# Key features from three full-height stacks a tile, and key norms given to ScalarE as a bias, in a random-feature attention block

## The chip, the cores and the metric

The kernel runs on one core of a Trainium2 chip. The metric is the time of one execution on the device in microseconds; 1303.4 us is the median of 3 runs of the kernel before (1302.08 to 1303.77). Traces are of one profiled execution.

## The reference

For each of 8 batches of 1024 tokens (512 channels, 16 heads of 32):

```python
def feature_map(x, orf):                       # orf: 128 x 32
    proj = x @ orf.T / d_k ** 0.25
    norm = jnp.sum(x * x, axis=-1, keepdims=True) / (2.0 * math.sqrt(d_k))
    return (jnp.exp(proj - norm) + EPS) / math.sqrt(m)
q = feature_map(split(x @ Wq.T + bq), orf)     # per head
k = feature_map(split(x @ Wk.T + bk), orf)
v = split(x @ Wv.T + bv)
kv, ksum = jnp.einsum('nlm,nld->nmd', k, v), jnp.sum(k, axis=1)
out = jnp.einsum('nlm,nmd->nld', q, concat(kv, ksum))
out = out[..., :-1] / out[..., -1:]
x = layernorm(x + merge(out) @ Wo.T + bo)
x = layernorm(x + x @ (ternary(weight) * scale).T)
```

The change touches only how `proj - norm` of the keys is formed.

## The kernel before

Every operand of a product is split into a rounded part (hi) and the rest (lo); a product is hi·hi + hi·lo + lo·hi, summed in PSUM.

A batch is worked off in 8 units and an output part. Unit `u` holds 4 heads (128 channels): even units are keys, odd ones queries. A key unit and the query unit behind it are called a pair below. All engines walk the same list, `SCHEDULE`, each taking the stages that concern it, in order and with semaphores between them. The stages that matter here:

- `P` (TensorE, L980): the projection of a unit two ahead, in parts of 6 products of 512 columns. A key unit has four parts: two before its middle, one behind it, one at its end.
- `S` (ScalarE, L668 and L670): writes the hi part of a projected half unit into `EH` ("unit_hi") and its squares. `L` (VectorE, L845) writes the lo part into `EL`. `Q` (VectorE, L853 and L857) turns and sums the squares; `N` (L863 to L868) makes norm rows of them.
- `LIFT` (SyncE's queue): copies the 32-row pieces of `EH` and `EL` from SBUF to SBUF into a stack, `ST`, which has one slot for keys and one for queries: 10 transfers for keys (L517, L523, L528), 12 for queries. The hi ones wait for `S` of the second half (L500) and for the last `F` of the unit before the last (L499), the lo ones for `L` (L525).
- `NL` (GpSimd's queue, L584 and L589): copies the norm rows into the same stack: 4 transfers for keys, 2 for queries.
- `F` (TensorE, called from L994 for keys with the product on L943, L999 for queries): the features of one tile. A key tile (128 tokens, 4 heads, 512 columns of one PSUM bank) is four products of 256 columns: for each pair of heads one against `MA` with 128 rows and one against `MB` with 68 rows, of which 4 carry the norms with a factor of -1. It goes round three PSUM banks, so `F` of a tile waits for the exponential of the tile three before. ScalarE (L687) takes the whole tile, 128x512, with one exponential into `FE`. `G` (TensorE, L1012) multiplies features by values, `KVT` and `GG` make use of the sums. VectorE also adds up the features (L809).
- `XT` (ScalarE, L655): splits the next batch's x, eight tiles, within unit 5. `LX` (SyncE, L439) loads those tiles; tiles 0 to 4 in unit 2, tiles 5 to 7 in unit 5. `LR` (SyncE, L461) loads rows of x.
- `ST` (ScalarE, L635 and L725): second layer norm and store of an output tile. Two of these lie in unit 0.

In a key unit other than 0 the list says, with the unit's own number `u`: `F` 0, 1; `P`; `F` 2, 3; `P`; `S` and `L` of the first half of unit `u+2`; `F` 4, 5; `Q`; `G` 0 to 3; `P`; `F` 6, 7; `S`, `L`, `Q` of its second half; `N`; `LIFT` and `NL` of unit `u+2`; `P`. In unit 2 the `LX` of five tiles stand behind that; in unit 5 those of three tiles stand behind the `LIFT` and `NL` of unit 6, which unit 4 ends with.

Of the kernel before, what the change touches and what calls it, by code (L numbers as in the profile page):

```python
# [44 lines left out]
P = 128  # L45
# [8 lines left out]
A_SQ = math.sqrt(1.0 / (2.0 * math.sqrt(DH)) / C_EXP)  # L54
QK = 3 * DH + 2
WARM = 24
KK = 2 * DH + 4
# [184 lines left out]
def attention_kernel(nc, x, xt, wq, wk, wv, wo, wff, bias, bo, orf, out):  # L242
# [5 lines left out]
    with ctx:  # L248
# [9 lines left out]
        ST = sb("stacks", [P, 2, 4 * L], F32R)  # L258
# [10 lines left out]
        MA = sb("orf_key_a", [P, 2 * M], F32R)  # L269
        MB = sb("orf_key_b", [P, 2, 2 * M], F32R)  # L270
# [4 lines left out]
        NN = sb("norm_rows", [P, 2, 2, DH], F32R)  # L275
# [48 lines left out]
        v_xlo, v_plo, v_n = Signal("x_lo_ready", 4, 4), Signal("unit_lo_ready", 2 * NU), Signal("norms_ready", 3 * NU, 2)  # L324
# [54 lines left out]
        masks = KVS[:, 0:2, :].rearrange("p a (b m) -> p (a b) m", m=M)  # L379
# [17 lines left out]
        def turned_rows(b, t):  # L397

            if b + 1 < B:
                return ST[:, 1, 2048:2560], ST[:, 1, 2560:3072]  # L400
            return last_hi[:, t, :], last_lo[:, t, :]
# [31 lines left out]
        def _(sp):  # L433
# [29 lines left out]
            for kind, b, at, _, _ in steps():  # L463
# [30 lines left out]
                elif kind == "LIFT":  # L494
                    u = at[0]
                    slot = ST[:, u % 2, :].bitcast(F32)
# [4 lines left out]
                    if u == 1:  # L501
# [10 lines left out]
                        continue  # L512
                    for h in range(HG):
                        src = hi[DH * h:DH * (h + 1), :]
                        if is_key(u):
                            r, c = 2 * DH * (h % 2), L * (h // 2)
                            sp.dma_start(slot[r:r + DH, c:c + L], src).then_inc(sig.sem, 16)  # L517
                        else:
                            sp.dma_start(slot[0:DH, L * h:L * (h + 1)], src).then_inc(sig.sem, 16)
                            sp.dma_start(slot[2 * DH:3 * DH, L * h:L * (h + 1)], src).then_inc(sig.sem, 16)  # L520
                    if is_key(u):
                        for p in range(2):
                            sp.dma_start(slot[0:2 * DH, L * (2 + p):L * (3 + p)],  # L523
                                         hi[2 * DH * p:2 * DH * (p + 1), :]).then_inc(sig.sem, 16)
                    wait(v_plo.sem, v_plo.nth(b, 2 * u + 2))  # L525
                    for h in range(HG):
                        r, c = (2 * DH * (h % 2) + DH, L * (h // 2)) if is_key(u) else (DH, L * h)
# [3 lines left out]
        def _(pool):  # L531
# [14 lines left out]
            for t in (WQS, MA, MB):  # L546
                last = nc.gpsimd.memset(t[:].bitcast(F32), 0.0)
# [567 lines left out]
```

## Time and profile before

| | us |
|---|---|
| median of 3 runs | 1303.4 |
| lowest and highest | 1302.08, 1303.77 |
| span of the profiled execution | 1300.4 |

The profiled execution's span runs from its first to its last instruction; its own time beyond it isn't recorded, and the median is 3.0 us above that span. The share of an engine's busy time says little here, since the work is a chain of stages with different limits. The profile is read in this order: the chain that ended last, for the engine that sets the end; the stretches from the start of one key unit's exponentials to the next one's; and then each engine's and each DMA queue's instructions in one such stretch in order of time.

### The profile page before, as it was taken

What the parts mean: (1) busy time and instruction counts of PE and PEld (TensorE: products, weight loads), DVE (VectorE), ACT (ScalarE), POOL (GpSimd) and SP (SyncE); (2) the same over time, 40 slices, a digit from 0 to 9 for tenths busy, and PEclk for the clock granted to TensorE, in tenths of its full rate; (3) what the DMA queues carried; (4) which work ended last, traced back from release to release, by engine and by line L of the source; (5) the groups of instructions that cost most, each with busy time, mean ns of one, the idle gap of its engine ahead of it and who ended that gap; (6) DMA issues with size and microseconds to landing.
All of it is one profiled execution on the core that took longest, in us unless ns stands there. A gap on an engine that the chain in (4) does not pass through costs nothing.

```text
span 1300.4 us, 24924 instructions
## 1 busy us (share of the span) xinstructions
PE 1280.2 (98%) x8626; PEld 965.9 (74%) x8626; DVE 942.1 (72%) x1784; ACT 702.1 (54%) x1403; POOL 384.1 (30%) x685
## 2 busy tenths in 40 slices
PE   9999999999999999999999999999999999999987
PEld 8767787777877678776787768876788767887665
DVE  7599765886668875787657786587875787657876
ACT  5557435564355743657336663367534665446534
POOL 1213432125311343214421234312352123422143
PEclk9999999999999999999999999999999999999999
DMA  7668414773146821567215762258612686026711
GB/s 242 140 136 217 95 50 111 170 190 84 57 118 160 200 68 54 133 159 189 62 57 130 182 165 69 62 130 197 162 45 71 142 209 149 30 80 147 163 51 65
DMA packets 83773, 160.56 MB, mean 123 GB/s; under 512 B 19648, under 2 KB 37184, under 8 KB 83136
## 3 DMA queue, kind: packets, MB, share of 16 engines
q1 hardware_dynamic: 67856, 139.78, 43.4%
q10 hardware_dynamic: 9648, 16.85, 3.4%
q0 software_dynamic: 6144, 2.34, 2.1%
q8 instruction: 69, 1.13, 0.4%
q14 instruction: 56, 0.46, 0.1%
HBM read 39.13 MB, written 16.78 MB: 43 GB/s over the span
## 4 chain that ended last, share of the span: by engine, by line
PE 84%; DVE 6%; ACT 6%; issue 3%; DMA 1%; POOL 0%; SPq 0%; ACTq 0%; DVEq 0%; POOLq 0%
PE ps L943 28%; PE ps L980 25%; PE ps L1044 8%; PE ps L1012 4%; PE ps L966 4%; PE ps L968 4%; PE ps L967 4%; PE ps L999 4%; ACT features L687 2%; PE ps L1070 2%; ACT x_hi L655 1%; DMA rows<-in_Wk_t 1%; DVE squares_turned L853 1%; ACT unit_hi L668 0%; DVE cols L857 0%
## 5 line engine op out<-in xcount | busy, mean ns | idle before, releaser
L687 ACT ACTIVATE features<-ps 128x512 f32<-128x512 f32 x512 | 279.0, 603 | 254.4 <-PE ps L943 196.0
L584 POOL DMA_DIRECT2D stacks<-norm_rows x128 | 86.3, 681 | 305.7 <-DVE norm_rows L868 185.8
L943 PE MATMUL ps<-Wo_hi,stacks 128*128 128x512 f32 x448 | 150.4, 402 | 0.0
L660 ACT ACTIVATE values_then_attention<-ps 128x512 f32<-128x512 f32 x64 | 38.3, 598 | 197.2 <-PE ps L968 194.1
L809 DVE TENSOR_TENSOR den<-den,features 128x512 f32<-128x512 f32 x186 | 128.0, 688 | 12.7
L562 POOL TENSOR_SCALAR stats<-stats 128x1 f32<-128x1 f32 x128 | 36.1, 282 | 323.4 <-DVE stats L796 323.2
L943 PE MATMUL ps<-orf_key_a,stacks 128*128 128x256 f32 x512 | 131.4, 288 | 0.1
L943 PE MATMUL ps<-orf_key_b,stacks 68*128 68x256 f32 x512 | 128.2, 282 | 0.0
L1044 PE MATMUL ps<-features,kv_ksum 128*32 128x512 f32 x1024 | 123.1, 598 | 3.4 <-ACT features L687 2.1
L845 DVE SCALAR_TENSOR_TENSOR unit_lo<-ps,cols,unit_hi 128x512 fp32r<-128x512 f32 x128 | 94.2, 736 | 35.0 <-ACT squares L670 34.9
L943 PEld LDWEIGHTS ps<-orf_key_a,stacks 128*128 128x128 f32 x512 | 97.1, 190 | 25.9 <-issue 22.1
L943 PE MATMUL ps<-W_ternary,stacks 128*128 128x512 f32 x448 | 110.7, 389 | 0.0
L980 PE MATMUL ps<-x_hi,Wk_hi 128*128 128x512 f32 x256 | 106.5, 416 | 1.4 <-DVE x_lo L838 1.4
L966 PE MATMUL ps<-Wv_hi,x_hi 128*128 128x512 f32 x256 | 102.6, 401 | 1.0 <-DVE unit_lo L845 0.2
L943 PEld LDWEIGHTS ps<-Wo_hi,stacks 128*128 128x128 f32 x448 | 84.1, 188 | 24.4 <-issue 7.1
L635 ACT ACTIVATE rows<-rows,stats 128x512 f32<-128x512 f32 x112 | 88.0, 813 | 26.4 <-POOL stats L566 25.6
L980 PE MATMUL ps<-x_lo,Wq_hi 128*128 128x512 f32 x256 | 101.3, 396 | 0.0
L980 PE MATMUL ps<-x_hi,Wq_hi 128*128 128x512 f32 x256 | 100.9, 394 | 0.0
L980 PE MATMUL ps<-x_hi,Wq_lo 128*128 128x512 f32 x256 | 100.7, 393 | 0.0
L980 PE MATMUL ps<-x_hi,Wk_lo 128*128 128x512 f32 x256 | 100.7, 393 | 0.0
L980 PE MATMUL ps<-x_lo,Wk_hi 128*128 128x512 f32 x256 | 100.4, 392 | 0.0
L967 PE MATMUL ps<-Wv_lo,x_hi 128*128 128x512 f32 x256 | 99.9, 390 | 0.0
(141 smaller groups left out, 2773.2 us busy)
## 6 DMA issues: line engine op xcount, KB each, us to landing
stacks<-unit_hi SPq DMA_DIRECT2D x384, 128.0 KB, 2.4
stacks<-unit_lo SPq DMA_DIRECT2D x256, 128.0 KB, 3.7
stacks<-unit_hi SPq DMA_DIRECT2D x64, 256.0 KB, 3.9
out<-rows ACTq DMA_DIRECT2D x56, 256.0 KB, 2.0
rows<-in_x_t SPq DMA_DIRECT2D x49, 256.0 KB, 4.5
rows<-in_x SPq DMA_DIRECT2D x32, 256.0 KB, 4.3
features<-in_x SPq DMA_DIRECT2D x32, 256.0 KB, 4.2
values_then_attention<-in_x_t SPq DMA_DIRECT2D x8, 256.0 KB, 7.1
```

Of the source, the lines that this page charges most:

```text
L584: pool.dma_start(slot[row:row + 2, c:c + L].rearrange("o (t c) -> o t c", c=DH), NN[2 * DH * p:2 * DH * (p + 1), u % 2, part, :].bitcast(F ...
L635: nc.scalar.activation(row, row, ACT.Identity, scale=ln(k, t, 10), bias=ln(k, t, 11))\
L687: nc.scalar.activation(FE[:, n % 8, :, 0:M], ps[:, :].rearrange("p (a m) -> p a m", a=HG), ACT.Exp, scale=C_EXP).then_inc(a_exp.sem, 1)
L809: ins = nc.vector.tensor_tensor(total, total, FE[:, r, :, 0:M], ALU.add)
L845: nc.vector.scalar_tensor_tensor(out=EL[:, u % 2, half], in0=ps[:, :], scalar=BC[:, u:u + 1], in1=EH[:, u % 2, half].bitcast(F32), op0=ALU ...
L943: last = mm(out, a, b, start=(n == 0), stop=(n == len(terms) - 1))
L966: mm(ps[:, :], XH[:, k, c], WH["v"][:, k, :], start=(k == 0), stop=False)
L967: mm(ps[:, :], XH[:, k, c], WL["v"][:, k, :], start=False, stop=False)
L968: last = mm(ps[:, :], XL[:, k, c], WH["v"][:, k, :], start=False, stop=(k == KT - 1))
L980: last = mm(ps[:, :], *terms[n], start=(n == 0), stop=(n == len(terms) - 1))
L999: last = mm(ps[:, :], WQS[0:QK, h, :], slot[0:QK, c:c + HALF], start=True, stop=True)
L1044: last = mm(bank[DH * h:DH * (h + 1), :], KVS[:, g % 2, c + DH * h:c + DH * (h + 1)], FE[:, HG * half + h, :, 0:M], start=True, stop=True, ...
```

## The change

The stack `ST` becomes two tensors, `KST` (3 x 1024 columns, keys) and `QST` (4 x 1024, queries). The twelve pieces that a key tile needs (hi, lo and hi again of four heads) are laid in three full stacks of 128 rows, and a tile takes three products of 256 columns against `MK`, whose outputs overlap by 128 columns. The norm rows of the keys leave the stack. `Q` of a key unit sums the squares with a minus sign into `KN`; `N` and GpSimd's `NL` are gone for keys. In their place SyncE's queue copies the sums by 16 transfers of 32 partitions x 8 numbers (32 bytes each) into `NB`, at the place of `NL`. ScalarE waits for these ahead of the first exponential of a key unit, and takes each tile by four exponentials of 128 columns, with a column of `NB` as bias. `A_SQ` becomes `A_KEY` for keys, since the norm is no longer scaled by `C_EXP`. Setup has fewer masks. `LIFT` of keys has 9 transfers instead of 10.

```diff
-        KEY_LIFTS, QUERY_LIFTS = 10, 12
+        KEY_LIFTS, QUERY_LIFTS = 9, 12
...
-        KEY_NORMS, QUERY_NORMS = 4, 2
+        KEY_NORMS, QUERY_NORMS = 16, 2
...
+                    if is_key(u):
+                        for n, r, h, k in ((0, 2 * DH, 0, 2), (1, DH, 1, 2), (2, 0, 2, 2), (0, 0, 0, 1), (2, 3 * DH, 3, 1)):
+                            sp.dma_start(slot[r:r + DH * k, L * n:L * (n + 1)], hi[DH * h:DH * (h + k), :]).then_inc(sig.sem, 16)
+                        wait(v_plo.sem, v_plo.nth(b, 2 * u + 2))
+                        for h, (n, r) in enumerate(((0, DH), (1, 0), (1, 3 * DH), (2, 2 * DH))):
+                            sp.dma_start(slot[r:r + DH, L * n:L * (n + 1)], lo[DH * h:DH * (h + 1), :]).then_inc(sig.sem, 16)
+                        continue
...
+                elif kind == "NL" and is_key(at[0]):
+                    u = at[0]
+                    wait(v_ns.sem, v_ns.nth(b, 2 * u + 2))
+                    if b or u:
+                        wait(a_exp.sem, a_exp.nth(b, 8 * (u - 1)))
+                    for h in range(HG):
+                        for a in range(4):
+                            sp.dma_start(NB[DH * a:DH * (a + 1), TT * h:TT * (h + 1)], KN[DH * h:DH * (h + 1), a, :]).then_inc(n_lifted[0].sem, 16)
...
-                if kind == "NL":
+                if kind == "NL" and not is_key(t):
                     lift_norms(b, t)
...
-                    nc.scalar.activation(FE[:, n % 8, :, 0:M], ps[:, :].rearrange("p (a m) -> p a m", a=HG),
-                                         ACT.Exp, scale=C_EXP).then_inc(a_exp.sem, 1)
+                    if is_key(u):
+                        if r == 0:
+                            norms_lifted(act, b, u)
+                        for h in range(HG):
+                            last = nc.scalar.activation(FE[:, n % 8, h, 0:M], ps[:, M * h:M * (h + 1)], ACT.Exp,
+                                                        bias=NB[:, TT * h + r:TT * h + r + 1], scale=C_EXP)
+                        last.then_inc(a_exp.sem, 1)
+                    else:
+                        nc.scalar.activation(FE[:, n % 8, :, 0:M], ps[:, :].rearrange("p (a m) -> p a m", a=HG),
+                                             ACT.Exp, scale=C_EXP).then_inc(a_exp.sem, 1)
...
+                    if is_key(u):
+                        if h == 0:
+                            norms_lifted(dve, b, u - 2)
+                        by_tile = KN[:, :, 4 * h:4 * (h + 1)].rearrange("p a t -> p t a")
+                        nc.vector.reduce_sum(by_tile, blocks.rearrange("p (t a) c -> p t a c", a=4),
+                                             axis=mybir.AxisListType.X, negate=True).then_inc(v_ns.sem, 1)
...
-                elif kind == "N":
+                elif kind == "N" and not is_key(u):
...
                     if is_key(u):
-                        for p in range(2):
-                            at_a, at_b = L * p + P * r, L * (2 + p) + P * r
-                            last = products(ps[:, 256 * p:256 * (p + 1)], [(slot[:, at_a:at_a + P], MA[:, :]),
-                                                                          (slot[0:KK, at_b:at_b + P], MB[0:KK, p, :])])
+                        for n in range(3):
+                            last = mm(ps[:, M * n:M * (n + 2)], KST[:, L * n + P * r:L * n + P * (r + 1)], MK[:, n, :],
+                                      start=(n == 0), stop=(n == 2), skip_group_check=True)
```

## Rows read from the trace of the kernel before

**Rows 1.** Page: busy time and share of the span; then the chain by engine
```profile
PE 1280.2 (98%) x8626; PEld 965.9 (74%) x8626; DVE 942.1 (72%) x1784; ACT 702.1 (54%) x1403; POOL 384.1 (30%) x685
...
PE 84%; DVE 6%; ACT 6%; issue 3%; DMA 1%; POOL 0%; SPq 0%; ACTq 0%; DVEq 0%; POOLq 0%
```

**Rows 2.** Stretches: A:B, length; busy PE, PEld, DVE, ACT, POOL; clock; DMA share; GB/s
```profile
524.92:547.46 22.54, 22.54 (x190) 16.00 (x189) 16.58 (x30) 15.58 (x33) 5.34 (x9) 1.00 0.63 144
547.46:571.24 23.78, 23.78 (x196) 17.05 (x195) 19.05 (x37) 14.25 (x31) 3.84 (x6) 1.00 0.71 175
571.24:596.56 25.32, 24.82 (x200) 17.71 (x199) 21.61 (x41) 18.45 (x40) 7.54 (x9) 1.00 0.75 183
596.56:620.39 23.83, 23.78 (x192) 16.80 (x190) 19.66 (x40) 15.89 (x35) 7.85 (x10) 1.00 0.59 146
...
1205.93:1229.43 23.50, 22.61 (x190) 16.07 (x189) 19.30 (x40) 14.27 (x32) 3.84 (x6) 1.00 0.66 142
```

**Rows 3.** Chain of waits in order, key unit 2: start us, length us, what
```profile
551.63 0.96 PE ps L943 x8
...
556.15 2.77 PE ps L980 x12
```

**Rows 4.** ScalarE in order of time, unit 2: start us, length us, instruction, idle before
```profile
547.46 1.09 ACT L687 ACTIVATE features<-ps 128x512 f32<-128x512 f32 x2 [3.96 <-PE ps L943]
...
556.68 0.69 ACT L668 ACTIVATE unit_hi<-ps,cols 128x512 fp32r<-128x512 f32 x1
557.25 0.70 ACT L670 ACTIVATE squares<-ps,cols 128x512 f32<-128x512 f32 x1
...
560.95 0.37 ACT L697 ACTIVATE kv_ksum_t<-ps,cols 128x128 f32<-128x128 f32 x1
561.22 0.19 ACT L697 ACTIVATION_READ_ACCUMULATOR kv_ksum_t<-ps,cols 128x1 f32 x1
```

**Rows 5.** SyncE's queue in order of time, units 2 to 5 (SPq: issue of transfers)
```profile
557.46 2.42 SPq L517 DMA_DIRECT2D stacks<-unit_hi  x4
...
561.26 2.87 SPq L528 DMA_DIRECT2D stacks<-unit_lo  x4
...
567.50 0.51 SPq L519 DMA_DIRECT2D stacks<-unit_hi  x1
...
585.04 2.90 SPq L528 DMA_DIRECT2D stacks<-unit_lo  x4
588.05 2.70 SPq L439 DMA_DIRECT2D rows<-in_x_t  x3
```

**Rows 6.** Page: DMA issues, KB each, median us to landing
```profile
stacks<-unit_hi SPq DMA_DIRECT2D x384, 128.0 KB, 2.4
```

**Rows 7.** VectorE, end of unit 4's squares (second half)
```profile
559.81 0.69 DVE L857 TENSOR_REDUCE cols<-squares_turned 128x16 f32<-128x512 f32 x1
```

**Rows 8.** ScalarE in order of time, unit 0 of the same batch
```profile
528.39 0.81 ACT L635 ACTIVATE rows<-rows,stats 128x512 f32<-128x512 f32 x1
...
529.77 1.09 ACT L687 ACTIVATE features<-ps 128x512 f32<-128x512 f32 x2 [0.57 <-PE ps L943]
```

**Rows 9.** ScalarE in order of time, last split of the next x, end of unit 5
```profile
596.02 0.63 ACT L655 ACTIVATE x_hi<-rows 128x512 fp32r<-128x512 f32 x1 [0.65 <-DMA rows<-in_x_t]
596.56 1.07 ACT L687 ACTIVATE features<-ps 128x512 f32<-128x512 f32 x2
```

**Rows 10.** ScalarE's own queue: issues of 32-byte rows at the start, and of a store
```profile
1.50 0.45 ACTq L621 DMA_DIRECT2D cols<-in_bias_columns  x1
1.98 0.45 ACTq L622 DMA_DIRECT2D den<-in_orf_t  x1
...
486.05 0.34 ACTq L725 DMA_DIRECT2D out<-rows  x1
```

**Rows 11.** ScalarE in order of time, the last key unit of the last batch
```profile
1229.43 3.05 ACT L687 ACTIVATE features<-ps 128x512 f32<-128x512 f32 x6 [3.12 <-PE ps L943]
```

**Rows 12.** A stretch near the end, columns as in rows 2: granted clock
```profile
1283.50:1293.00 9.50, 7.89 (x30) 6.13 (x31) 6.06 (x11) 4.51 (x7) 2.90 (x8) 0.82 0.15 55
```

More of the change, by code:

```diff
@@ L513, in _ @@
                     for h in range(HG):
                         src = hi[DH * h:DH * (h + 1), :]
[L515 to L520, printed above, removed]
@@ L578, in lift_norms @@
                     wait(t_ff.sem, t_ff.nth(b, 0))
-                wait(v_n.sem, v_n.nth(b, 3 * u + 3))
+                wait(v_n.sem, v_n.nth(b, 3 * (u // 2) + 3))
                 for part in range(2):
-                    if is_key(u):
-                        for p in range(2):
-                            row, c = 2 * DH + 2 * part, L * (2 + p)
-                            pool.dma_start(slot[row:row + 2, c:c + L].rearrange("o (t c) -> o t c", c=DH),
-                                           NN[2 * DH * p:2 * DH * (p + 1), u % 2, part, :].bitcast(F32))\
-                                .then_inc(n_lifted[0].sem, 16)
-                    else:
-                        row = 3 * DH + part
-                        pool.dma_start(slot[row:row + 1, :].rearrange("o (t c) -> o t c", c=DH),
-                                       NN[:, u % 2, part, :].bitcast(F32)).then_inc(n_lifted[1].sem, 16)
+                    row = 3 * DH + part
+                    pool.dma_start(slot[row:row + 1, :].rearrange("o (t c) -> o t c", c=DH),
+                                   NN[:, part, :].bitcast(F32)).then_inc(n_lifted[1].sem, 16)
             for kind, b, at, _, _ in steps():
                 t = at[0] if at else 0
-                if kind == "NL":
+                if kind == "NL" and not is_key(t):
                     lift_norms(b, t)
@@ L755, in constant_rows @@
                         nc.vector.tensor_copy(WQS[DH * r:DH * (r + 1), h, :], wT[DH * r:DH * (r + 1), 0:M])
-                for r in range(4):
-                    a = r // 2
-                    nc.vector.tensor_copy(MA[DH * r:DH * (r + 1), M * a:M * (a + 1)], wT[DH * r:DH * (r + 1), 0:M])
+                for n, r, a in ((0, 0, 0), (0, 1, 0), (0, 3, 1), (1, 0, 0), (1, 2, 1), (1, 3, 1), (2, 1, 1), (2, 2, 1)):
+                    nc.vector.tensor_copy(MK[DH * r:DH * (r + 1), n, M * a:M * (a + 1)], wT[DH * r:DH * (r + 1), 0:M])
                 link(nc.vector.tensor_copy(rounded, wT[:, 0:M]))
@@ L763, in constant_rows @@
                     nc.vector.tensor_tensor(WQS[r, h, :], wT[r, 0:M], rounded[r, :].bitcast(F32), ALU.subtract)
-                for p in range(2):
-                    for a in range(2):
-                        r = slice(DH * a, DH * (a + 1))
-                        nc.vector.tensor_tensor(MB[r, p, M * a:M * (a + 1)], wT[r, 0:M], rounded[r, :].bitcast(F32), ALU.subtract)
-                nc.vector.tensor_copy(WQS[3 * DH:QK, :, :], masks[3 * DH:QK])
-                last = nc.vector.tensor_copy(MB[2 * DH:KK, :, :].rearrange("p a (b m) -> p (a b) m", b=2), masks[2 * DH:KK])
-                last.then_inc(s_orf, 1)
+                for n, q, a in ((0, 2, 0), (1, 1, 0), (2, 0, 0), (2, 3, 1)):
+                    r = slice(DH * q, DH * (q + 1))
+                    nc.vector.tensor_tensor(MK[r, n, M * a:M * (a + 1)], wT[r, 0:M], rounded[r, :].bitcast(F32), ALU.subtract)
+                nc.vector.tensor_copy(WQS[3 * DH:QK, :, :], minus_one).then_inc(s_orf, 1)
             def weight_scale():
@@ L998, in _ @@
                         c = L * h + HALF * half
-                        last = mm(ps[:, :], WQS[0:QK, h, :], slot[0:QK, c:c + HALF], start=True, stop=True)
+                        last = mm(ps[:, :], WQS[0:QK, h, :], QST[0:QK, c:c + HALF], start=True, stop=True)
                     last.then_inc(t_f.sem, 1)
```

76 lines of the change are left out of this document (36 added, 40 removed).

## Prediction

> **What bounds the kernel now.** I read the chain of waits by engine first: TensorE is on it for 84% of the span and busy for 98% [rows 1], so in most stretches a product taken away moves the end. Then I read the stretches from one key unit's first exponential to the next one's: TensorE is busy for all 23.78 us of the second, ScalarE for 14.25, and only in the third does TensorE wait a little, behind the splitting of x [rows 2]. Last I followed one key unit on ScalarE and on SyncE's queue in order of time [rows 4, 5]. The reader is to see there that ScalarE has room and that SyncE's queue, which no busy column shows, issues one transfer per 0.6 us: 4 in 2.42 us [rows 5]. That queue is what the change loads.
>
> **TensorE, removed.** Two key tiles, 8 products of 256 columns, take 0.96 us on the chain [rows 3], 0.12 us a product. Three instead of four saves 0.12 us a tile, 0.96 us a key unit, and over 8 batches x 4 key units x 8 tiles 30.7 us, if TensorE still sets the pace. The overlapping outputs change no column count.
>
> **ScalarE, added.** One exponential of 128x512 is replaced by four of 128x128 with a bias column. Two whole ones take 1.09 us, so about 0.50 us a tile [rows 4]. The trace has no 128-column exponential; nearest is the 128x128 activation with a bias column, behind which the next instruction starts 0.27 us later (560.95 to 561.22) [rows 4]. The 512-column one with bias is followed after 0.57 us (556.68 to 557.25) [rows 4]; taking the share of 384 columns off it, at 0.50/512 us a column, leaves 0.20 us. I take 0.26, near the row of the same size: 1.04 us a tile, 8.3 a key unit instead of 4.0. Bounds: 0.20 and 0.30. In unit 2 ScalarE's work in a pair goes from 14.25 to about 18.6 us of 23.78 [rows 2], so it fits on average; in unit 0 two stores lie there too, each holding ScalarE from 528.39 to 529.77 [rows 8].
> The Trainium skill ("ScalarE: Activation LUTs", What ACT_TABLE_LOAD costs) gives about 280 ns + 0.833 ns a column with a pointer bias and an overlap of 93 ns, which for 128 columns is an estimate of 0.29 us apart, near my upper bound; by it the time below would be about 23 us higher.
>
> **VectorE and GpSimd, removed.** `N` of keys (three small instructions) and GpSimd's four transfers a key unit go. Neither is on the chain beyond a few per cent [rows 1], so I cost them at nothing. The sum with a minus sign has the same 512 inputs; nothing there.
>
> **SyncE's queue, added, and the new wait.** `LIFT` of keys loses one transfer (0.61 us), and 16 follow it for the norms. They stand ahead of the `LX` transfers and of the query unit's `LIFT` (12 transfers, 7.3 us), and ScalarE's exponentials of the key unit wait for the last of them; behind that wait stand all of ScalarE's work, then the three PSUM banks, then TensorE. What does one cost? The trace has no such small SBUF-to-SBUF transfer on this queue. Lifts cost 0.51 alone and 0.61 in a train (2.42 for 4, and the gap) [rows 5]; 128 rows of 32 bytes on ScalarE's queue 0.45, 0.48 apart; a store of 256 KB 0.34 [rows 10]. Size thus doesn't order these prices, kind of transfer may: I take the lifts' 0.62, with 0.36 (a store and a gap) as the low end and 0.68 as the high. Landing: 2.3 us from the issue as for a lift [rows 6].
>
> **The loop that this closes.** Set 0 at the first exponential of key unit u (2 or 4), where it had been waiting. Eight tiles, 8.3 us, and `S` of the first half, 1.14, come ahead of `S` of the second half, whose hi part ends 0.69 after its start: 10.15. In the kernel before that start lay at 9.2 (547.46 to 556.68), and the queue began 0.1 after the hi part [rows 4, 5]. `LIFT` took 6.67 us for 10 transfers (557.46 to 561.26 + 2.87) [rows 5]; 9 take 6.06, so 16.3. The sums are ready sooner: 3.8 us behind the start of `S` before (556.68 to 559.81 + 0.69) [rows 4, 7], so at 13.3. Fifteen distances of 0.62 and one landing, 9.3 + 2.3, and 0.2 for the semaphores: 28.1 us until the first exponential of unit u+2. The pair took 23.78 before, and would take 22.8 by TensorE. So the saved 0.96 us vanishes and 4.3 us are added, in an idle TensorE.
>
> **By pairs of a batch.**
> - Unit 0 to 2: two tiles, `S`, two tiles, a store, one tile bring 7.6 us; tile 7 gets its bank and is done at about 8.2, then one more tile and `S` end at 9.4. Hence 9.5 + 6.06 + 11.8 = 27.3 against 22.54 [rows 2]: +4.8.
> - Unit 2 to 4: +4.3.
> - Unit 4 to 6: 28.1 isn't the end here. The `LX` of tiles 5 to 7 come behind the norms: 10.25 + 6.06 + 9.9 + 0.2 = 26.4 after the start. Before, the exponentials of unit 6 followed their issue by 8.5 us (588.05 to 596.56, behind the last split of x) [rows 5, 9]. So 34.9 against 25.32 [rows 2]: +9.6. The five `LX` of unit 2 push unit 5's `LIFT` by 3 us, which ends inside this.
> - Unit 6 to the next batch: no key unit waits there for norms before the output part is over. TensorE's saving is eaten by the late start, the rest has cover: 0.
> That is 18.7 us a batch, for 7 batches 131. The last has no x to load: 4.8 + 4.3 + (28.1 - 23.50 = 4.6) [rows 2], and its last key unit, where six exponentials take 3.05 us in a row [rows 11], adds some 3.5 net: 17. The first batch's norms (16 behind `LIFT` 0) are done in the prologue, under the projections. The sum is 148 us: span 1300.4 + 148 = 1448.4, and with the 3.0 us by which the median lies above the span 1451 us.
>
> **The clock.** TensorE will stand for 4 to 9 us ahead of three key units a batch. Near the end of the trace, after gaps, the granted clock was 0.82 over 9.5 us, that is 1.2 GHz instead of 2.4 for 3.4 of them, a loss of 1.7 us [rows 12]. After each wait ScalarE, not TensorE, sets the pace, so I take nothing; if each of the 24 waits cost 1.7, it would be 41 us.
>
> **Rivals.**
> 1. *Small transfers are cheap to issue.* At 0.36 us apart a train is 3.9 us shorter: pairs of +0.9, +0.4, +5.5, and 6 in the last batch: 53 us, 1357. For it: the 0.34 of a store; against it: each SBUF-to-SBUF issue in the trace took over 0.5.
> 2. *The norms arrive in time,* by landing alone. Then unit 0 is held by ScalarE: with 1.04 us a tile TensorE waits for banks there some 3 us in all (a store between tiles 3 and 4), +2.0, and three pairs gain 0.96 or less: about 1303. The loop allows this if it is under 22.8, that is if a distance is under 0.27 us.
> The Trainium skill ("DMA: Bandwidth & Descriptors", Issuing engines are not separate DMA queues) calls the issue time "usually small relative to the DMA itself"; by that rule the train would cost hardly more than one landing, which is this rival. The rows stand against it: 0.6 us each, times 16, is four times a landing.
> 3. *Faster, as the removal of products promises.* Same point, 0.27 us a distance, and a short exponential at 0.20, so that unit 0 keeps up: all 30.7 us come in, 1273. Against it: no queue row is under 0.33.
> 4. *Worse than the loop:* 0.68 a distance (+0.9 a loop), 0.30 an exponential (+0.04 x 32, 1.3 a loop) and the clock's 1.7 a wait together: 1451 + 24 x 3.9 = 1545; two of the three, 1490 to 1520.
>
> **How the numbers follow.** Forecast 0.68 (1395 to 1490: distance 0.45 to 0.68, a short exponential 0.24 to 0.30), rival 1 0.14 (1345 to 1395), rival 2 0.05, rival 3 0.04, rival 4 0.09. Leaving out rivals 2 to 4 leaves out 0.18, so the range is 1345 to 1490. Differences under 0.2%, 2.6 us, can't be told from none: faster 0.06 (rival 3 and a part of 2), same 0.03, slower 0.91.
>
> **What would show it.** In the trace after: three products a key tile, 0.36 us a tile; 16 transfers a key unit on SyncE's queue, 0.6 us apart; ScalarE's idle time ahead of the first key exponential ended by DMA, 4 to 9 us; first exponentials of units 2 and 4 some 28 us apart, of 4 and 6 some 35; the output part as long as before. TensorE busy share well under 98%. It's wrong if the distances are under 0.45 us, if key exponentials are over 0.3 apart, or if ScalarE's waits end by TensorE.

## The result and the profile after

The changed kernel took 1474.9 us (median of 4 runs, 1470.3 to 1477.7), the kernel before, run beside it, 1303.6 us: a ratio of 1.1315 [1.129, 1.1339]. The forecast was 1451, with a range from 1345 to 1490.

Page of the kernel after: span, busy time, the chain by engine and by line, the costliest group, and the issues of the new transfers. To be read against [rows 1]. A line number is always that of the kernel whose profile is shown, so one and the same instruction has other numbers in other kernels.

```profile
span 1475.4 us, 25377 instructions
...
PE 1305.1 (88%) x8370; PEld 969.1 (66%) x8370; DVE 942.7 (64%) x1692; ACT 833.8 (57%) x2171; POOL 294.8 (20%) x553
...
PE 52%; SPq 24%; ACT 10%; issue 5%; DMA 4%; DVE 3%; ACTq 0%; POOL 0%; POOLq 0%; DVEq 0%
PE ps L951 16%; SPq L534 15%; PE ps L988 11%; ACT features L687 7%; SPq L515 5%; PE ps L1001 4%; PE ps L974 4%; PE ps L976 4%; PE ps L975 4%; SPq L518 4%; PE ps L1019 2%; DMA key_bias<-key_norms 2%; DMA rows<-in_x_t 2%; PE ps L1051 2%; PE ps L1077 2%
...
L687 ACT ACTIVATE features<-ps,key_bias 128x128 f32<-128x128 f32 x1024 | 277.4, 422 | 209.3 <-DMA key_bias<-key_norms 145.8
...
key_bias<-key_norms SPq DMA_DIRECT2D x512, 1.0 KB, 1.7
```

TensorE has 256 products fewer and is busy for 25 us more. Its share of the chain fell from 84% to 52%, and SyncE's queue, which was at 0%, has 24%, of which 15 are the norm transfers (L534) and 9 the key lifts (L515, L518). ScalarE stood for 145.8 us ahead of key exponentials until a norm transfer landed.

Stretches of the kernel after, the same batch as [rows 2]; the first three run from one key unit's first exponential to the next one's, the fourth is key unit 6 with half of unit 7, the fifth the output part. The last two lines lie around the wait of unit 4.

```profile
590.08:618.25 28.17, 24.79 (x192) 16.64 (x190) 19.76 (x36) 19.56 (x58) 2.92 (x6) 1.00 0.35 92
618.25:648.36 30.11, 24.56 (x186) 17.35 (x186) 19.39 (x34) 18.36 (x56) 1.70 (x4) 0.92 0.50 110
648.36:684.12 35.76, 25.54 (x186) 17.71 (x186) 21.52 (x37) 22.66 (x63) 3.77 (x3) 0.83 0.63 166
684.12:708.46 24.34, 23.11 (x178) 16.11 (x178) 17.27 (x27) 20.00 (x59) 5.28 (x5) 0.92 0.55 147
708.46:771.57 63.11, 63.00 (x294) 51.63 (x294) 37.99 (x73) 21.82 (x36) 23.52 (x51) 1.00 0.21 61
636.00:649.00 13.00, 8.00 (x54) 4.12 (x53) 8.53 (x18) 2.79 (x7) 1.07 (x2) 0.93 0.19 40
649.55:656.00 6.45, 6.45 (x50) 5.43 (x51) 3.52 (x5) 6.36 (x22) 0.00 (x0) 0.66 1.00 261
```

The three pairs take 28.2, 30.1 and 35.8 us where [rows 2] have 22.5, 23.8 and 25.3; the forecast had 27.3, 28.1 and 34.9. From the first exponential of unit 6 to that of the next batch it is 87.45 us (24.34 + 63.11), before it was 87.07 in that batch. TensorE's clock, 1.00 in all of [rows 2], is 0.92, 0.83 and 0.92 in the stretches behind a wait.

The 16 norm transfers of a key unit, which SyncE issues in a row, are called the train below. One loop in order of time, SyncE's queue between the first exponentials of units 2 and 4, to be read against [rows 5]:

```profile
629.53 3.46 SPq L515 DMA_DIRECT2D key_stack<-unit_hi  x5
633.11 2.47 SPq L518 DMA_DIRECT2D key_stack<-unit_lo  x4
635.77 10.88 SPq L534 DMA_DIRECT2D key_bias<-key_norms  x16
646.77 1.93 SPq L439 DMA_DIRECT2D rows<-in_x_t  x4
```

And ScalarE in the same loop, to be read against [rows 4] (in brackets the idle time before, and what ended it):

```profile
618.25 4.23 ACT L687 ACTIVATE features<-ps,key_bias 128x128 f32<-128x128 f32 x16 [7.56 <-DMA key_bias<-key_norms]
...
626.69 2.17 ACT L687 ACTIVATE features<-ps,key_bias 128x128 f32<-128x128 f32 x8 [0.99 <-PE ps L1001]
628.70 0.74 ACT L664 ACTIVATE unit_hi<-ps,cols 128x512 fp32r<-128x512 f32 x1
...
648.36 4.23 ACT L687 ACTIVATE features<-ps,key_bias 128x128 f32<-128x128 f32 x16 [10.21 <-DMA key_bias<-key_norms]
```

The loop closes as foretold: exponentials, the hi part at 628.70, nine lifts from 629.53, sixteen norm transfers from 635.77, landing, exponentials at 648.36. Sixteen exponentials in 4.23 us with the last 0.42 long lie (4.23 - 0.42)/15 = 0.254 us apart.

### The profile page after: what moved, and what is told of

Read it like the earlier page. It is cut to its first block, busy times and chain, and to the rows that moved or that the text cites. A ratio compares the mean times of both kernels' runs of the same rounds, so it can differ in the third digit from the quotient of the medians.

```text
span 1475.4 us, 25377 instructions
## 1 busy us (share of the span) xinstructions
PE 1305.1 (88%) x8370; PEld 969.1 (66%) x8370; DVE 942.7 (64%) x1692; ACT 833.8 (57%) x2171; POOL 294.8 (20%) x553
## 3 DMA queue, kind: packets, MB, share of 16 engines
q1 hardware_dynamic: 91920, 140.33, 37.3%
## 4 chain that ended last, share of the span: by engine, by line
PE 52%; SPq 24%; ACT 10%; issue 5%; DMA 4%; DVE 3%; ACTq 0%; POOL 0%; POOLq 0%; DVEq 0%
PE ps L951 16%; SPq L534 15%; PE ps L988 11%; ACT features L687 7%; SPq L515 5%; PE ps L1001 4%; PE ps L974 4%; PE ps L976 4%; PE ps L975 4%; SPq L518 4%; PE ps L1019 2%; DMA key_bias<-key_norms 2%; DMA rows<-in_x_t 2%; PE ps L1051 2%; PE ps L1077 2%
## 5 line engine op out<-in xcount | busy, mean ns | idle before, releaser
L687 ACT ACTIVATE features<-ps,key_bias 128x128 f32<-128x128 f32 x1024 | 277.4, 422 | 209.3 <-DMA key_bias<-key_norms 145.8
L1001 PE MATMUL ps<-orf_key,key_stack 128*128 128x256 f32 x768 | 141.1, 318 | 139.6 <-ACT features L687 139.6
L1001 PEld LDWEIGHTS ps<-orf_key,key_stack 128*128 128x128 f32 x768 | 125.1, 216 | 179.1 <-ACT features L687 146.8
L691 ACT ACTIVATE features<-ps 128x512 f32<-128x512 f32 x256 | 139.8, 618 | 21.9 <-PE ps L1006 17.8
L951 PE MATMUL ps<-Wo_hi,query_stack 128*128 128x512 f32 x448 | 150.3, 402 | 0.0
L585 POOL DMA_DIRECT2D query_stack<-norm_rows x64 | 35.3, 554 | 445.6 <-DVE norm_rows L876 389.2
L951 PE MATMUL ps<-W_ternary,query_stack 128*128 128x512 f32 x448 | 110.7, 389 | 0.0
L988 PE MATMUL ps<-x_lo,Wk_hi 128*128 128x512 f32 x256 | 110.3, 431 | 0.0
L951 PEld LDWEIGHTS ps<-Wo_hi,query_stack 128*128 128x128 f32 x448 | 84.1, 188 | 24.4 <-issue 7.1
L976 PE MATMUL ps<-Wv_hi,x_lo 128*128 128x512 f32 x256 | 99.9, 390 | 0.0
```

The lines of the kernel that those rows point to most:

```text
L687: last = nc.scalar.activation(FE[:, n % 8, h, 0:M], ps[:, M * h:M * (h + 1)], ACT.Exp, bias=NB[:, TT * h + r:TT * h + r + 1], scale=C_EXP)
L691: nc.scalar.activation(FE[:, n % 8, :, 0:M], ps[:, :].rearrange("p (a m) -> p a m", a=HG), ACT.Exp, scale=C_EXP).then_inc(a_exp.sem, 1)
L951: last = mm(out, a, b, start=(n == 0), stop=(n == len(terms) - 1))
L976: last = mm(ps[:, :], XL[:, k, c], WH["v"][:, k, :], start=False, stop=(k == KT - 1))
L988: last = mm(ps[:, :], *terms[n], start=(n == 0), stop=(n == len(terms) - 1))
L1001: last = mm(ps[:, M * n:M * (n + 2)], KST[:, L * n + P * r:L * n + P * (r + 1)], MK[:, n, :], start=(n == 0), stop=(n == 2), skip_group_ch ...
```

## The experiments

Each time is the median of 4 to 10 runs, beside runs of the kernel before, whose median there was between 1302.8 and 1303.4. "Pairs" below are the three stretches from key unit to key unit in the fourth of the 8 batches, and from unit 6 to the next batch, in this order; before they are 22.54, 23.78, 25.32 and 87.07, after 28.17, 30.11, 35.76 and 87.45. The last two are best read as a sum: in five of the first seven batches of the kernel before they are 24.6 and 87.8, with the same 112.4 together. The code cuts are against the changed kernel unless another is named, and `...` marks lines left out.

The theory is the forecast's: a place on SyncE's queue is the price, by the wait for the last norm and by what stands behind the train. Its rivals: ScalarE's short exponentials, the landing of a transfer, TensorE's clock. The first three kernels add the parts of the change one by one.

**1. Three products alone.** The norms, their transfers and the four short exponentials go.

```diff
-                    for h in range(HG):
-                        for a in range(4):
-                            sp.dma_start(NB[...], KN[...]).then_inc(n_lifted[0].sem, 16)
...
-                        for h in range(HG):
-                            last = nc.scalar.activation(FE[:, n % 8, h, 0:M], ps[:, M * h:M * (h + 1)], ACT.Exp,
-                                                        bias=NB[:, TT * h + r:TT * h + r + 1], scale=C_EXP)
+                        nc.scalar.activation(FE[:, n % 8, :, 0:M], ps[:, :].rearrange("p (a m) -> p a m", a=HG),
+                                             ACT.Exp, scale=C_EXP).then_inc(a_exp.sem, 1)
```

> The stacks and three products of the change alone: one exponential of 512 columns a key tile as before, no norm transfers, no wait. The key norms are left out of the computation. Theory A (the products are worth what TensorE's chain says, and the loss is all in what came with them): 0.96 us a key unit, 30.7 us in all, 1273 us; a little less where the splitting of the next x sets unit 5, 1273 to 1281. Rival B (the three overlapping products are themselves slower, or TensorE loses elsewhere): 1300 or more.

Measured: 1288.3 us, ratio 0.9881 [0.9865, 0.9897], 14.5 us under before and outside what was expected. Pairs 21.80, 22.80, 23.61 and 88.46. The first two give 0.7 and 1.0 us. The last two together took 112.4 us before and 112.1 here, so they give 0.3 where twice 0.96 had been reckoned. What is lost there is taken up in 5.

**2. With the four short exponentials,** bias zero, no transfers. As in 1, SyncE's branch for the key norms is gone too.

```diff
-                        if r == 0:
-                            norms_lifted(act, b, u)
```

> As the run of three products alone, but each key tile takes four exponentials of 128 columns with a bias column that is zero from the start; the key norms are left out of the computation. Nothing is transferred and nothing waits. Theory A: only unit 0, where two stores lie, is held by ScalarE (about 3 us a batch), and the last key unit: about 1303, 1295 to 1310. Rival C (the doubled work of ScalarE is a main cause of the loss): 1340 or more.

Measured: 1313.7 us, 1.008 [1.0062, 1.0097], 25.4 more than the kernel in 1 and 4 us over what was expected. Pairs 24.47, 22.80, 23.61 and 88.59: short exponentials cost nothing in pairs two and three, as the forecast had it, and 2.7 us in the first, where two output stores also lie on ScalarE (3.3 in the first batch, where ScalarE splits a weight there instead). The last key unit of all has 2.8 more (9.6 instead of 6.8 us to the query's first exponential).

**3. With the transfers, unwaited.** The kernel of 2 with all 16 transfers a key unit, into a tile that nobody reads.

```diff
+        NB2 = sb("unread_bias", [P, HG * TT])
...
-                            sp.dma_start(NB[...], KN[...]).then_inc(n_lifted[0].sem, 16)
+                            sp.dma_start(NB2[...], KN[...]).then_inc(n_lifted[0].sem, 16)
```

> As the run with short exponentials and a zero bias (key norms left out of the computation), but SyncE's queue also issues the 16 small transfers at their place, into a tile that nobody reads; ScalarE doesn't wait for them. It tells the time that they take in the queue from the wait for them. Theory A (the queue is full: what stands behind the 16, the query unit's 12 lifts and the loads of x, comes late too): pairs of units 2 and 4 together 12 us longer, about 1400, 1375 to 1425. Rival D (it is ScalarE's wait for the last small transfer alone): as without them, about 1303.

Measured: 1427.9 us, 1.0949 [1.0924, 1.0974]. So 114.2 us come from the train's place on the queue alone, with no wait for a norm, and the wait adds only the last 46 or so, to 1474.9. The shares hold in this order of adding: where the queue sets the pace, it covers what the short exponentials cost in 2. Stretches of this kernel:

```profile
572.45:596.93 24.48, 22.79 (x182) 15.03 (x181) 16.35 (x27) 19.61 (x58) 2.48 (x5) 1.00 0.40 105
596.93:623.90 26.97, 24.52 (x188) 16.92 (x187) 18.48 (x34) 18.36 (x55) 1.06 (x2) 0.94 0.52 120
623.90:658.99 35.09, 27.00 (x198) 18.61 (x196) 24.08 (x45) 22.72 (x63) 4.86 (x5) 0.90 0.65 168
```

ScalarE in order of time in pairs two and three, its waits for query features:

```profile
610.77 1.09 ACT L693 ACTIVATE features<-ps 128x512 f32<-128x512 f32 x2 [3.00 <-PE ps L1008]
...
641.10 1.09 ACT L693 ACTIVATE features<-ps 128x512 f32<-128x512 f32 x2 [6.35 <-PE ps L1008]
```

SyncE's queue in pair three:

```profile
642.28 10.45 SPq L535 DMA_DIRECT2D unread_bias<-key_norms  x16
653.15 1.32 SPq L440 DMA_DIRECT2D rows<-in_x_t  x3
```

Without the wait the query units are late instead: their 12 lifts stand behind the train, and TensorE's query features (L1008) wait for them. And the three loads of x stand behind the train of unit 6, so the third pair is still 35.09 us long (32.4 to 38.5 over the first seven batches).

**4. Half the transfers,** all else as in the change.

```diff
-                        for a in range(4):
+                        for a in range(2):
```

> The changed kernel with 8 of the 16 norm transfers of a key unit; the other half of the bias tile stays zero, so half of the key norms are left out of the result. Theory A (ScalarE waits for the last of the train, so each transfer less is worth its place on SyncE's queue): the train was 10.0 to 10.9 us for 16, so 8 fewer take 5.0 to 5.4 us off each loop that goes through it. First pairs 27.9 - 5.1 is below what the four short exponentials allow without any transfer (24.5), so 24.5; second 30.0 - 5.3 = 24.7; third 35.5 - 5.3 = 30.2. Together -14 us a batch, 98 for seven, some 7 to 9 for the last: 1475 - 106 = about 1369, range 1355 to 1385. Theory B (a fixed wait for the norms' landing costs, not the number of transfers): unchanged but for a few tenths of a microsecond a unit, above 1460.

Measured: 1353.3 us, 1.0377 [1.0361, 1.0392], 2 us better than the better end of theory A's range; B is out. The pairs are 24.45, 24.14 and 28.59: the first is at the floor that ScalarE sets (2), and the third came out 1.6 us better than reckoned (27.1 to 31.6 over the first seven batches). Eight transfers less, 256 in all, gave 121.6 us.

**5. GpSimd held in its place.** The kernel of 1, in which GpSimd waits where it used to issue the key norms' transfers; the norms are still left out.

```diff
-                if kind == "NL" and not is_key(t):
+                if kind == "NL" and is_key(t):
+                    wait(v_ns.sem, v_ns.nth(b, 2 * t + 2))
+                elif kind == "NL":
                     lift_norms(b, t)
```

> Three products a key tile, one exponential of a whole tile, key norms left out of the result, and GpSimd held at the place where it used to issue the key norms' transfers until VectorE has summed the key squares. Theory A (without that hold GpSimd starts its adds of the output bias early, beside VectorE's adds of features, both take over twice their time, and TensorE waits 1.4 us at the end of each batch): the long feature adds (1.65 us) go back to 0.7, the stretch from unit 6 to the next batch goes from 87.6 to about 86.8 us, 7 x 0.9 to 1.4 off 1288.3: about 1280, range 1277 to 1283. Theory B (GpSimd's order has no part in it, the longer adds have another cause): 1288, within 2 us.

Measured: 1279.7 us, 0.9821 [0.9804, 0.9837], as theory A had it. Pairs 21.82, 22.82, 23.60, 87.29. The gain over the kernel of 1 lies in the last stretch of each batch, and the lines show how it comes about. In the kernel of 1, behind the start of unit 6, GpSimd's adds of the output bias:

```profile
593.86 3.37 POOL L597 TENSOR_TENSOR rows<-rows,out_bias 128x512 f32<-128x512 f32 x2 [0.65 <-DMA rows<-in_x]
```

VectorE's adds of features in that kernel:

```profile
593.71 2.38 DVE L798 TENSOR_TENSOR den<-den,features 128x512 f32<-128x512 f32 x2
596.68 1.89 DVE L798 TENSOR_TENSOR den<-den,features 128x512 f32<-128x512 f32 x2
```

And TensorE's wait for the lo part of a projected half:

```profile
596.81 0.50 PE L974 MATMUL ps<-x_hi,Wq_hi 128*128 128x512 f32 x1 [1.16 <-DVE unit_lo L834]
```

With GpSimd held, at the same place, GpSimd's adds:

```profile
599.30 2.52 POOL L599 TENSOR_TENSOR rows<-rows,out_bias 128x512 f32<-128x512 f32 x2 [8.97 <-DVE key_norms L849]
```

VectorE's:

```profile
590.83 1.49 DVE L800 TENSOR_TENSOR den<-den,features 128x512 f32<-128x512 f32 x2
592.89 1.48 DVE L800 TENSOR_TENSOR den<-den,features 128x512 f32<-128x512 f32 x2
```

TensorE's wait:

```profile
593.03 0.50 PE L976 MATMUL ps<-x_hi,Wq_hi 128*128 128x512 f32 x1 [0.28 <-DVE unit_lo L836]
```

Side by side, two bias adds take 3.37 us instead of 2.52 and two feature adds up to 2.38 instead of 1.49, which delays VectorE's lo part, for which TensorE waits. In all, 12 of the 186 feature adds take over 1 us in the kernel of 1, and none in the kernel before or with GpSimd held. The change drops GpSimd's key `NL`, and with it the wait that kept those adds out of VectorE's crowded stretch; in the changed kernel 8 feature adds take over 1 us.

**6. Two queues.** All 16 transfers, 8 issued by SyncE and 8 by GpSimd.

```diff
+                if kind == "NL" and is_key(t):
+                    wait(v_ns.sem, v_ns.nth(b, 2 * t + 2))
+                    if b or t:
+                        wait(a_exp.sem, a_exp.nth(b, 8 * (t - 1)))
+                    for h in range(HG):
+                        for a in range(2, 4):
+                            pool.dma_start(NB[...], KN[...]).then_inc(n_rest.sem, 16)
```

> The whole changed kernel, all 16 norm transfers of a key unit, but 8 of them issued by SyncE at their old place and 8 by GpSimd, which waits for the same sums. Theory A (the price is a place on one engine's queue): GpSimd issued the old norms' transfers 0.6 to 0.67 us apart, so both halves are out after 5 to 5.5 us, side by side, and the kernel runs like the one with 8 transfers, 1353, or up to 10 us less, since GpSimd held at its old place no longer adds beside VectorE: range 1340 to 1365. Theory B (the transfers themselves, or the DMA engines under both queues, set the 0.6 us): the 16 still land some 10 us after the first is issued, 1475, range 1455 to 1485.

Measured: 1347.1 us, 1.0342 [1.0305, 1.038]: theory A. GpSimd's issues ahead of unit 6:

```profile
583.57 3.92 POOL L599 DMA_DIRECT2D key_bias<-key_norms  x8 [9.45 <-DVE key_norms L871]
```

And SyncE's:

```profile
586.50 4.94 SPq L537 DMA_DIRECT2D key_bias<-key_norms  x8
```

Here each engine issues its eight in 4 to 5 us, GpSimd 2.9 us ahead, so that all 16 are out after 7.9 us. The number of transfers is that of the changed kernel, and 127.8 of its 171.3 us are gone (holding GpSimd again is worth up to the 9 us of 5 of them). So neither the transfers' bytes nor their landing cost that time, but their places in a row on one queue.

**7. TensorE kept at work.** The changed kernel, with unused products ahead of the feature tile at which TensorE stands.

```diff
+                if kind == "F" and u in FILL and at[1] == 3 and (b, u) != (B - 1, NU - 2):
+                    for _ in range(FILL[u]):
+                        mm(PS[nb][:, :], WH["k"][:, 0, 0:P], WH["q"][:, 0, :], start=True, stop=True)
```

> The changed kernel, with TensorE kept at work while it waits: ahead of feature tile 3 of units 2, 4 and 6 it computes 8, 20 and 34 products of 512 columns into the bank that the next projection product overwrites; their result is not used. Theory A (the half-speed products after the wait delay the next unit's projection, its lift and so the next norms, 1.0 to 1.5 us a loop): 1.0 us off the third pair's and the second pair's loop and 1.5 off the last, 2.5 to 4 us a batch: 1475 - 8 x 3 = about 1451, range 1443 to 1460. Theory B (the loop is paced by ScalarE's exponentials after the wait and by the queue, TensorE catches up): within 3 us of 1475. If the products outlast the wait, slower.

Measured: 1460.8 us, 1.1212 [1.1187, 1.1237], 14 us less than the changed kernel, 0.8 us above theory A's range, and well clear of B. Its stretches:

```profile
587.95:616.96 29.01, 26.68 (x200) 18.00 (x198) 20.21 (x36) 19.56 (x57) 3.54 (x7) 1.00 0.35 90
616.96:645.67 28.71, 27.52 (x206) 19.74 (x206) 18.75 (x33) 18.13 (x56) 1.07 (x2) 1.00 0.50 115
645.67:679.28 33.61, 30.78 (x219) 22.06 (x219) 21.32 (x37) 22.45 (x63) 3.83 (x3) 1.00 0.63 171
```

The clock is 1.00 throughout. Pair two is 1.4 and pair three 2.2 us shorter than in the change; pair one, which begins without such a wait, gained nothing. The gain is where it had been expected: the lifts of pair two begin 10.18 us after its start, instead of 11.28 in the changed kernel, and those of pair three 10.18 instead of 11.74.

```profile
627.14 3.43 SPq L516 DMA_DIRECT2D key_stack<-unit_hi  x5
```

So the clock is a real but small part, about 14 of 171 us. That is a net figure: in two batches the stretch behind unit 6, which also has unused products, was 1.2 and 2.5 us longer than in the change.

**8. The norms moved by VectorE,** 16 copies of 32x8 behind the squares of a key unit, no transfer; SyncE's branch for them is gone.

```diff
+                elif kind == "N" and is_key(u):
+                    dve.wait_ge(v_ns.sem, v_ns.nth(b, 2 * u + 2))
+                    if b or u:
+                        dve.wait_ge(a_exp.sem, a_exp.nth(b, 8 * (u - 1)))
+                    for h in range(HG):
+                        for a in range(4):
+                            nc.vector.tensor_copy(NB[...], KN[...]).then_inc(n_lifted[0].sem, 1)
```

> The whole changed kernel, with VectorE instead of SyncE moving the norms across partitions: 16 copies of 32x8 elements right behind the last query or key projection's norms. Theory A (only the queue and the wait cost; VectorE has room, 64% busy): 1313.7, the time of the kernel with short exponentials and no transfer, and 8 to 30 us for 16 copies of 0.1 to 0.2 us in each of 31 key units as far as they are not in idle time: range 1305 to 1335. Theory B (VectorE, held in its order until the exponentials of the unit before have read the old bias, passes its adds and residuals on late, TensorE waits for unit_lo): 1335 to 1380.

Measured: 1346.0 us, 1.0333 [1.0303, 1.0363], in theory B's range, but not by its wait. Pairs 24.45, 22.78, 24.00 and 92.66: against 2 the copies cost at most 0.4 us in three places and 4 us in the fourth (in the first batch 1.3 to 2.7 in the other three as well). VectorE there:

```profile
625.77 2.56 DVE L802 TENSOR_TENSOR den<-den,features 128x512 f32<-128x512 f32 x2
...
635.58 3.07 DVE L865 COPY key_bias<-key_norms 32x8 f32<-32x8 f32 x16
638.68 0.42 DVE L879 COPY kv_ksum<-ps 128x256 f32<-128x256 f32 x1
```

VectorE has idle time in other stretches, but none here from 619.7 to 639.9 us; the adds of features, stretched again by GpSimd, come first, then 3.07 us of copies, and behind them the copy of the sums that the last products of the unit need. TensorE stood for 25.9 us in all for that copy (`kv_ksum`), and for 6.9 for `unit_lo`, which theory B had named. In this batch it stood 2.40 us, and behind that the granted clock was 0.52, so that the next 16 products took 3.58 us instead of 1.92:

```profile
639.16:642.74 3.58, 3.58 (x17) 0.65 (x17) 0.73 (x1) 0.00 (x0) 0.00 (x0) 0.52 0.00 0
```

**9. The norms moved by GpSimd,** 16 copies in a chain, at its old `NL`; SyncE's branch for them is gone.

```diff
+                if kind == "NL" and is_key(t):
+                    ...
+                            nc.gpsimd.tensor_copy(NB[...], KN[...]).then_inc(n_lifted[0].sem, 1)
```

> The whole change, with the 16 transfers of key norms taken off SyncE's queue: GpSimd, which is idle there, copies the same 16 blocks from tile to tile itself, one behind the other. All is computed. Theory A (the train of transfers on SyncE's queue is the cause): 16 copies of about 0.4 us end at 13.3 + 6.4 = 19.7 us of a loop that allows 22.8, so the wait is hidden: 1303, 1295 to 1310, as with short exponentials and no norms. Rival C: 1340 or more.

Measured: 1304.9 us, 1.0013 [1.0003, 1.0022]: the same work as the change, 170 us faster. Pairs 24.45, 22.82, 24.00, 86.58. Sixteen copies took 5.08 us ahead of unit 6 (3.84 ahead of unit 4), and no engine waited for them. GpSimd in order of time:

```profile
586.96 5.08 POOL L593 COPY key_bias<-key_norms 32x8 f32<-32x8 f32 x16 [8.09 <-DVE key_norms L867]
```

It is also 8.8 us faster than the kernel of 2, which computes no norms at all; the copies hold GpSimd in its place, as in 5. What is left over the kernel of 5 is the first pair, 24.45 instead of 21.82, the first batch's, 26.82 instead of 22.03, and the last key unit, 9.6 instead of 6.7.

**10. The stores of unit 0 moved to unit 1,** in the kernel of 9; the cut is against that kernel.

```diff
-        st = [[("ST", b - 1, t)] if u == 0 and b else [] for t in (TT - 2, TT - 1)]
+        st = [[], []]
...
+            st = [[("ST", b - 1, t)] if u == 1 and b else [] for t in (TT - 2, TT - 1)]
+            seq += kv + f(2, 3) + st[0] + p[1] + [("KVT", b, g)] + s0 + l0 + f(4, 5) + st[1] + p[2] + ...
```

> The version in which GpSimd copies the norms and the queue is left alone, with the last two output stores of a batch issued by ScalarE in unit 1 instead of unit 0. Theory A (its first pair, 24.5 us against 22.8 and 23.6 in the others, is longer because unit 0 has both 32 short exponentials and two stores on ScalarE): first pair 21.8 to 22.8, so -1.7 to -2.7 us for seven batches: 1304.9 - 15 = about 1290, range 1285 to 1294. Theory B (the first pair is longer for the lifts and loads of its place, or for GpSimd's copies): within 3 us of 1305.

Measured: 1298.9 us, 0.9964 [0.9951, 0.9977], 5 us short of theory A's range: the first pair went to 23.53 us only. In the middle of unit 1 the stores delay the query's exponentials: TensorE waited for them.

```profile
543.51 0.49 PE L1013 MATMUL ps<-query_stack,orf_query 98*128 98x512 f32 x1 [0.93 <-ACT features L698]
```

**11. The same, both stores behind the last squares of unit 1;** the cut is against the kernel of 10.

```diff
-            seq += kv + f(2, 3) + st[0] + p[1] + ... + f(4, 5) + st[1] + p[2] + f(6, 7) + s1 + q0 + ...
+            seq += kv + f(2, 3) + p[1] + ... + f(4, 5) + p[2] + f(6, 7) + s1 + st[0] + st[1] + q0 + ...
```

> The version with GpSimd's copies and the stores in unit 1, with both stores (each a scaled row tile of 0.83 us and an issue) moved behind the last square of unit 1, where ScalarE had 2.5 us idle before the next key unit's exponentials. Theory A (in unit 1's middle the stores held back squares and exponentials, TensorE waited 0.9 us for features, and the first pair stayed at 23.55 us): first pair 22.0 to 22.8, 7 x 0.8 to 1.5 us off 1298.9: about 1291, range 1287 to 1294. Theory B (what is left of the first pair over 21.8 is ScalarE's own 16 short exponentials a tile pair, whatever stands in unit 1): within 2 us of 1299. Theory C (the stores now end later than the next unit's exponentials can start): 1300 to 1308.

Measured: 1290.3 us, 0.9905 [0.9891, 0.9918], so this version is 1% faster than the kernel before. Its stretches:

```profile
522.93:545.31 22.38, 22.12 (x182) 15.04 (x181) 16.17 (x27) 19.66 (x58) 5.42 (x21) 1.00 0.50 125
545.31:568.11 22.80, 22.80 (x188) 16.06 (x187) 18.46 (x34) 18.41 (x56) 4.02 (x18) 1.00 0.73 196
568.11:591.72 23.61, 23.11 (x188) 16.07 (x187) 20.30 (x37) 22.48 (x64) 8.60 (x21) 1.00 0.74 188
591.72:678.70 86.98, 86.82 (x482) 68.29 (x481) 57.87 (x110) 41.90 (x94) 31.91 (x73) 1.00 0.31 86
```

TensorE is busy again in 154.85 of these 155.77 us. The norms and all 32 short exponentials a key unit are in it, and it lies 10.7 us over the kernel of 5, which has neither; 5.9 of them are the first pair of the first batch (27.9 instead of 22.0 us), 3.8 the last key unit of all, where no other work lies beside ScalarE (10.5 instead of 6.7 us to the query's first exponential).

## Why the prediction was right, and where its terms were off

Laid out by runs, each against before: three products -23.7 us; GpSimd no longer held +9.2; four short exponentials +25.4; the train's place on the queue +114.2; the wait for its last landing +46.2. Together +171, where the forecast had 148. The span grew by 175.0 us, 154.4 of them up to the first exponential of the last batch (forecast 131) and 20.6 behind it (17). By pairs, over the seven batches:

| | forecast | measured |
|---|---|---|
| unit 0 to 2 | 33.6 | 37.3 |
| unit 2 to 4 | 30.1 | 41.6 |
| unit 4 to 6 | 67.2 | 73.8 |
| unit 6 to the next batch | 0 | 1.8 |

The mechanism was right: the wait and its loop came as told. Every stretch took somewhat more than forecast, and the loop from unit 2 to 4 the most.

- *TensorE, removed.* The three products take 0.12 us each as before, and the pairs in which TensorE sets the pace give 0.98 us (23.78 to 22.80). Of 30.7 us 23.7 are to be had: less in the first pair (0.7), 0.5 to 0.8 behind unit 6, 0.2 to 0.3 in the second and third pair of the first batch, and nothing in the last batch's third pair (23.50 in both). In the change itself the saving disappears in waits, as forecast.
- *ScalarE.* 0.26 us apart foretold, 0.254 measured; 1.02 us a tile. The estimate of 0.29 worked out from the Trainium skill ("ScalarE: Activation LUTs", What ACT_TABLE_LOAD costs) was above what the trace shows. In the second and third pair the short exponentials are free, by experiment 2. The forecast had the first pair, too, wait for the queue and not for ScalarE; that held with 16 transfers (28.17 against 24.47), not with 8.
- *VectorE and GpSimd, removed at no cost.* This step was wrong. VectorE's work had been on 6% of the chain and GpSimd's on none of it [rows 1], but the wait in front of GpSimd's key `NL` had kept its adds away from VectorE's. Without it 9 us are lost in experiment 1. The step took no account of what a deleted wait had held back, and experiment 5 shows it. In the changed kernel the price was not measured by itself; the version with two queues, which holds GpSimd again, is 6 us faster than the one with eight transfers, but it also differs in the other queue.
- *SyncE's queue.* 0.62 us a place was right: 0.59 an issue, most starts 0.63 apart. What was missed is the irregular long one: one issue of 1.47 us in the train of unit 4, 1.83 for the longest of the 512, and 18 of them over 1 us. They came often enough to count, since a train is 16 in a row: 10.88 us for the 16 issues from 635.77 on, where 15 x 0.62 + 0.59 makes 9.9. The trains took 10.0 to 11.3 us. The landing was 1.7 in the median instead of 2.3; from the start of the last issue of unit 4's train, at 646.1, to the exponential it was 2.2.
- *The loop, 28.1 foretold, 30.11 measured.* From the first exponential of unit 2 the lifts began after 11.28 us instead of 10.25, since ScalarE stood 0.99 us for a feature tile ahead of tiles 6 and 7; `LIFT` took 6.24 instead of 6.06; from the train's start to the exponential it was 12.59 instead of 11.8. These are +1.0, +0.2 and +0.8.
- *The clock, taken at nothing.* This is the 1.0. Three feature tiles fit into the three PSUM banks; ahead of the fourth TensorE stands until ScalarE has freed a bank. In unit 2 it stood 2.86 us, and behind that the products of the next projection lay 0.43 us apart, not 0.23 (granted clock 0.63 from 619.44 to 624.00). In unit 4, which begins the next loop, it stood 5.55 us and the products lay 0.43 apart again; the granted clock was 0.66 over the 6.45 us behind that gap, so it was at 1.2 GHz for 4.4 of them. TensorE in order of time in the kernel after:

```profile
619.44 0.68 PE L1001 MATMUL ps<-orf_key,key_stack 128*128 128x256 f32 x3 [2.86 <-ACT features L687]
619.92 0.63 PE L988 MATMUL ps<-x_hi,Wk_hi 128*128 128x512 f32 x1
620.35 0.63 PE L988 MATMUL ps<-x_hi,Wk_lo 128*128 128x512 f32 x1
...
649.55 1.01 PE L1001 MATMUL ps<-orf_key,key_stack 128*128 128x256 f32 x3 [5.55 <-ACT features L687]
650.36 0.63 PE L988 MATMUL ps<-x_hi,Wk_hi 128*128 128x512 f32 x1
650.79 0.63 PE L988 MATMUL ps<-x_hi,Wk_lo 128*128 128x512 f32 x1
```

  The argument that ScalarE sets the pace behind each wait was wrong: the projection between the feature tiles is on the loop, and at the lower clock ScalarE waits for tile 6 behind it. With the clock kept up in experiment 7 the lifts begin after 10.18 us, which is the forecast's 10.25. The size is 14 us in all, nearer to nothing than to the bound of 41.
- *Unit 4 to 6, +9.6.* Measured 35.76, forecast 34.9. That this is so near is luck, since errors cancel: the lifts began after 11.74 us instead of 10.25 and took 7.47 instead of 6.06, the train 10.4 instead of 10.1, and from the first `LX` to the exponential it was 6.1 instead of 8.5. And the base was an odd one, 25.3 instead of 24.6, which only two of the seven batches have; pair and what follows it took 112.4 us before and 123.2 after in this batch, +10.8.
- *Unit 0 to 2,* 27.3 foretold, 28.17 measured; *unit 6 to the next batch,* 0 foretold, +0.4 in this batch.
- *Rivals.* Cheap issue was near 1357, which is what eight transfers gave; its condition, 0.36 us a place, no row shows. That the norms come in time didn't hold: sixteen issues took 10.0 to 11.3 us against a landing of 1.7. The Trainium skill's sentence ("DMA: Bandwidth & Descriptors", Issuing engines are not separate DMA queues) that issue is usually small beside the DMA itself doesn't fit these transfers: one issue, 0.59 us, is a third of a landing, and in a row the issues add up while the landings overlap. With the queue left alone the kernel took 1304.9, which is that rival's 1303, reached in another way.

## What to carry to other kernels

Count small SBUF-to-SBUF transfers by places on their queue, not by bytes: here each cost 0.6 us to everything that stood behind it, needed or not, and the same move by an engine with idle time, or halved over two queues, took 128 to 170 of the 171 us back. When a step is deleted, look at what its wait kept in order on its engine; an instruction that runs earlier isn't free if it shares something with the engine that is crowded then. And a saving is worth what the engine with the least room in that very stretch allows: two stores moved by one unit were worth 15 us.

## What the runs showed of the hardware that was not expected

- VectorE and GpSimd slow each other. A 128x512 fp32 add of two SBUF tiles takes VectorE 0.69 us (at most 0.695 in the kernel of experiment 5) and up to 1.67 us beside the same kind of add on GpSimd, whose own pair goes from 2.52 to 3.37 us.
- An issue of a norm transfer on SyncE's queue is 0.59 us in the median, but between 0.51 and 1.83, with 18 of 512 over 1 us.
- Three waits of TensorE, of 2.40 us (experiment 8), 2.86 and 5.55 us (the changed kernel, units 2 and 4), were followed by a granted clock of 0.52 over 3.58, 0.63 over 4.56 and 0.66 over 6.45 us. Such a wait costs more than its length where TensorE's work is on the loop: 4 us for the one of 2.40.
- GpSimd moves a 32x8 block across partitions, each copy waiting for the one before, in 0.24 to 0.32 us (3.84 and 5.08 for 16); VectorE takes 0.19 (3.07 for 16).
- GpSimd's queue issued the same transfers 0.49 us apart (3.92 for 8), SyncE's 0.62 (4.94 for 8).
